# Counting edges on one NeuronCore: a block's digit sum in three pieces between places, its bytes parted one place sooner, GpSimd's staged edges in a ring of eight

## What is computed

```python
deg = jnp.maximum(segment_sum(ones, dst, num_segments=3125), 1.0)
deg_isqrt = deg ** (-0.5)
h = jnp.maximum(_layernorm(x), 0.0)
for i in range(10):
    agg = segment_sum(feat[src] * (d[dst] * d[src])[:, None], dst)
    feat_p = agg * 0.9 + 0.1 * h
    feat = feat_p * layer_reg[i] + (1.0 - layer_reg[i]) * feat
x = x + feat
h = jnp.maximum(_layernorm(x), 0.0)
for _ in range(4):
    m = (h @ W_msg.T + b_msg).reshape(n, 4, 128)
    r = segment_sum(m[src, edge_type], dst)
    h = gru_cell(r, h, w_ih, w_hh, b_ih, b_hh)
x = x + h
```

## Time and profile before

| | us |
|---|---|
| median of 3 runs | 2418.93 |
| lowest and highest of the 3 | 2417.05, 2979.36 |
| the profiled execution, its time | 2416.61 |
| its span in the profile | 2415.0 |
| one-hot places, first to last (in the span) | 39.35 to 423.54 |
| last digit sum ends | 439.87 |

### The profile page before, as it was taken

How to read it: one execution, slowest core, us unless ns; L and a number is a source line. 1 busy time by engine, 2 the same in 40 slices (tenths; PEclk the granted TensorE clock), 3 DMA queues, 4 the chain that set the end, 5 groups by cost and what they waited for, 6 DMA issues and landing times.

```text
span 2415.0 us, 40583 instructions
## 1 busy us (share of the span) xinstructions
PE 2159.3 (89%) x14377; PEld 1405.2 (58%) x14888; DVE 1384.7 (57%) x2714; ACT 505.5 (21%) x1122; POOL 235.7 (10%) x517
## 2 busy tenths in 40 slices
PE   4545555699999999999999999999999999999998
PEld 3223223599998989889544565444654446544465
DVE  8878778787777767787822347223463224542243
ACT  4877778400000000000300103000031000210010
POOL 4645555000000000000000000000000000000000
PEclk9565655699999999999999999999999999999999
DMA  2000000100000000005100000000000000010000
GB/s 77 22 33 22 22 33 22 50 2 1 2 2 2 2 2 1 2 1 151 47 1 1 1 1 1 1 1 1 1 1 1 1 1 1 1 27 1 1 1 28
DMA packets 23056, 34.26 MB, mean 14 GB/s; under 512 B 2573, under 2 KB 18939, under 8 KB 22466
## 3 DMA queue, kind: packets, MB, share of 16 engines
q1 hardware_dynamic: 19897, 30.56, 3.8%
q10 hardware_dynamic: 2944, 0.93, 0.2%
HBM read 18.04 MB, written 13.45 MB: 13 GB/s over the span
## 4 chain that ended last, share of the span: by engine, by line
PE 77%; DVE 9%; ACT 7%; issue 4%; ACTq 1%; DVEq 1%; POOL 0%; POOLq 0%; DMA 0%
PE ps L819 43%; PE ps L898 26%; PE ps L802 4%; ACT weighed L538 3%; PE ps L786 2%; ACT packed L531 2%; ACT words L520 1%; ACTq L511 1%; DVE marks L1093 1%; DVE dig L1121 1%; DVE big L1123 1%; PE ps L748 1%; DVEq L1080 1%; PE ps L883 1%; PE ps L704 1%
## 5 line engine op out<-in xcount | busy, mean ns | idle before, releaser
L819 PE MATMUL ps<-slots,m_parts 125*128 125x500 fp8e4 (+1 forms) x5600 | 1083.3, 353 | 1.5 <-DVE slots L1398 1.0
L819 PEld LDWEIGHTS ps<-slots,m_parts 125*128 125x128 f16 x5600 | 546.4, 98 | 487.5
L898 PE MATMUL ps<-parts,big 125*128 125x256 f16 x6125 | 669.5, 273 | 6.2 <-DVEq L1469 6.2
L898 PEld LDWEIGHTS ps<-parts,big 125*128 125x128 fp8e4 x6125 | 591.3, 98 | 63.5
L1398 DVE TENSOR_SCALAR slots<-big 128x3200 int32<-128x3200 int32 (+1 forms) x112 | 244.2, 2183 | 281.7 <-PE ps L819 281.6
L704 PE MATMUL ps<-hot_pair,weighed 125*128 125x228 f16 x1000 | 210.4, 359 | 180.8 <-ACT weighed L538 96.5
L704 PEld LDWEIGHTS ps<-hot_pair,weighed 125*128 125x128 f16 x1000 | 113.3, 120 | 277.9 <-ACT weighed L538 240.1
L538 ACT ACTIVATE weighed<-marks,win_w 125x128 f16<-125x128 f16 x625 | 195.6, 389 | 90.0 <-DVE marks L1093 89.0
L1526 DVE SCALAR_TENSOR_TENSOR r_parts<-ps,over,r_parts 128x500 f16<-128x500 f32 (+1 forms) x28 | 19.1, 684 | 229.7 <-ACT r_parts L615 229.7
L1533 DVE SCALAR_TENSOR_TENSOR gate_r<-ps,over,gate_r 128x500 f32<-128x500 f32 (+1 forms) x28 | 19.1, 681 | 226.6 <-PE ps L802 226.6
L477 ACT ACTIVATE rs<-rs 125x25 f32<-125x25 f32 (+3 forms) x5 | 1.1, 216 | 703.0 <-DVE rs L971 703.0
(11 more groups left out here) (204 smaller groups left out, 1328.8 us busy)
## 6 DMA issues: line engine op xcount, KB each, us to landing
packed_counts<-packed SPq DMA_DIRECT2D x16, 625.0 KB, 2.9
big<-packed_counts SPq DMA_DIRECT2D x4, 1600.0 KB, 7.6
big<-packed_counts SPq DMA_DIRECT2D x3, 1200.0 KB, 6.4
hd<-in_x SPq DMA_DIRECT2D x1, 1562.5 KB
x_again<-in_x SPq DMA_DIRECT2D x1, 1562.5 KB
big<-x_after_hops SPq DMA_DIRECT2D x1, 1400.0 KB
x_after_hops<-x SPq DMA_DIRECT2D x4, 224.0 KB
out<-big SPq DMA_DIRECT2D x4, 224.0 KB
```

The lines of the kernel that those rows point to most:

```text
L819: last = pe.matmul(ps[:, k % 2, 0:SIZES[k] * Q], m_parts[0:Q, a, h, t * F:(t + 1) * F], slots_f8[0:Q, t % 2, 0:SIZES[k], a, 0:Q], start=a ...
L898: last = pe.matmul(ps[:, n % RING, 0:2 * F], tot_f8[0:Q, c, a, :], both((parts0, parts1)[par], a), start=a == 0, stop=a == TILES - 1)
```

## The change

Three things are changed.

1. `sum_digits` is cut into three pieces, `part` (the wait for the lanes and two instructions), `add` (one instruction) and `place` (two). Within a block they are issued behind the places j = 5, 6 and 7, where all five instructions stood behind place 6. The last two blocks, summed behind all places, keep them in a row.
2. ACT parts the three lanes behind the places 2, 3 and 4, not 3, 4 and 5. In the last block the third lane moves into the block accordingly.
3. POOL's four tiles get eight buffers (`WINDOWS`). The first eight places are staged without a wait; from then on place q waits for PE to be done with place q - 8. POOL's loop has eight places in a pass, and the wait stands ahead of the register load. The one-hots keep their four buffers, which is why `onehots` and `weigh` now take two indices, b for these and v for the staged tiles.

```diff
--- before.py
+++ after.py
@@ -63,6 +63,7 @@
 TWOS, NIBBLES = 0x33333333, 0x0f0f0f0f
 BANKS = 8
 DEPTH = 4
+WINDOWS = 8
 ROUND = 4
 WA = 5
 WD = W - WA
@@ -169,10 +170,10 @@
-            win_key = sb("win_key", [128, DEPTH, W, 2], F16, b)
-            win_place = sb("win_place", [128, DEPTH, W, 2], F16, b)
-            win_f = sb("win_f", [128, DEPTH, W, 2], F16, b)
-            win_w = sb("win_w", [128, DEPTH, W], F32, b)
+            win_key = sb("win_key", [128, WINDOWS, W, 2], F16, b)
+            win_place = sb("win_place", [128, WINDOWS, W, 2], F16, b)
+            win_f = sb("win_f", [128, WINDOWS, W, 2], F16, b)
+            win_w = sb("win_w", [128, WINDOWS, W], F32, b)
             win_p = sb("win_p", [128, 2, W], F16, b)
             win_x = sb("win_x", [128, 3], F32, b)
             hot_pair_x = sb("hot_pair_x", [128, KP], F16, b)
@@ -395,7 +396,6 @@
 
             def stage_window(q, b):
                 lo = pool.value_load(windows[0:1, ds(q, 1)], min_val=0, max_val=NCH)
-                pool.wait_ge(s_hot_used, q + 1)
 
                 def twice(m):
                     return m.rearrange("p (w o) -> p w o", o=1).broadcast_to([CH, W, 2])
@@ -407,11 +407,15 @@
                                    q_off[0:CH, ds(q, 1)].rearrange("p (w o) -> p w o", o=1).broadcast_to([CH, W, 2]),
                                    ALU.subtract).then_inc(s_wst, 1)
 
-            with pool.Fori(0, Q // DEPTH) as i:
-                for j in range(DEPTH):
-                    stage_window(DEPTH * i + j, j)
-            for q in range(Q // DEPTH * DEPTH, Q):
-                stage_window(q, q % DEPTH)
+            for q in range(WINDOWS):
+                stage_window(q, q)
+            with pool.Fori(1, Q // WINDOWS) as i:
+                for j in range(WINDOWS):
+                    pool.wait_ge(s_hot_used, WINDOWS * (i - 1) + j + 1 + DEPTH)
+                    stage_window(WINDOWS * i + j, j)
+            for q in range(Q // WINDOWS * WINDOWS, Q):
+                pool.wait_ge(s_hot_used, q - WINDOWS + 1 + DEPTH)
+                stage_window(q, q % WINDOWS)
 
             pool.wait_ge(s_bnd, 1)
             pool.partition_all_reduce(mbound[:, 6:7], mbound[:, 5:6], 128, bass.bass_isa.ReduceOp.max).then_inc(s_bndr, 1)
@@ -532,22 +536,22 @@
                 if l == LANES - 1:
                     ins.then_inc(s_bytes, 1)
 
-            def weigh(q, b):
+            def weigh(q, b, v):
                 act.wait_ge(s_marks, q + 1)
                 for w in range(WA):
                     act.activation(weighed[0:CH, b, w, :], marks[0:CH, b, w, :], ACT.Copy,
-                                   scale=win_w[0:CH, b, w:w + 1]).then_inc(s_weighed, 1)
+                                   scale=win_w[0:CH, v, w:w + 1]).then_inc(s_weighed, 1)
 
             def block_of(turn, b, n, turn_before):
                 blk = 2 * turn + b
                 for j in range(n):
-                    weigh(BQ * blk + j, j % DEPTH)
+                    weigh(BQ * blk + j, j % DEPTH, j % WINDOWS)
                     if j >= 2:
                         evacuate(blk, b, j - 2)
                     elif turn_before is not None:
                         evacuate(2 * turn_before + 1 - b, 1 - b, BQ - 2 + j)
-                    if 3 <= j < 3 + LANES and turn_before is not None:
-                        part_lane(turn_before, 1 - b, j - 3, 16 * turn_before + BQ * (1 - b) + BQ - 1)
+                    if 2 <= j < 2 + LANES and turn_before is not None:
+                        part_lane(turn_before, 1 - b, j - 2, 16 * turn_before + BQ * (1 - b) + BQ - 1)
 
             block_of(0, 0, BQ, None)
             with act.Fori(0, (NB - 2) // ROUND) as i:
@@ -560,7 +564,6 @@
                 block_of(turn + 1, 0, BQ, turn)
             block_of(NB // 2 - 1, 1, Q - (NB - 1) * BQ, NB // 2 - 1)
             evacuate(NB - 1, 1, 3)
-            part_lane(NB // 2 - 1, 0, 2, BQ * (NB - 1) - 1)
             evacuate(NB - 1, 1, 4)
             for l in range(LANES):
                 part_lane(NB // 2 - 1, 1, l, Q - 1)
@@ -1075,7 +1078,7 @@
             dve.sem_inc(s_mp, 1)
             dve.sem_inc(s_ct, 1)
 
-            def onehots(q, b):
+            def onehots(q, b, v):
 
                 many = dve.value_load(windows[0:1, ds(q + MANY, 1)], min_val=0, max_val=NCH)
                 dve.wait_ge(s_wst, q + 1)
@@ -1091,12 +1094,12 @@
                     return m.rearrange("p w (o two) -> p w o two", o=1).broadcast_to([CH, count, n // 2, 2])
 
                 TT(by_two(marks[0:CH, b, :, :], 128), row(iota_row[0:CH, :], W, 128),
-                   each(win_place[0:CH, b, :, :], W, 128), ALU.is_equal).then_inc(s_marks, 1)
+                   each(win_place[0:CH, v, :, :], W, 128), ALU.is_equal).then_inc(s_marks, 1)
                 TT(by_two(hot_pair[0:CH, b, :, :], KP), row(iota_pair[0:CH, :], W, KP),
-                   each(win_key[0:CH, b, :, :], W, KP), ALU.is_equal).then_inc(s_pairs, 1)
+                   each(win_key[0:CH, v, :, :], W, KP), ALU.is_equal).then_inc(s_pairs, 1)
                 dve.wait_ge(s_marks, q + 1)
                 TT(by_two(weighed[0:CH, b, WA:W, :], 128), by_two(marks[0:CH, b, WA:W, :], 128),
-                   each(win_f[0:CH, b, WA:W, :], WD, 128), ALU.mult).then_inc(s_weighed_d, 1)
+                   each(win_f[0:CH, v, WA:W, :], WD, 128), ALU.mult).then_inc(s_weighed_d, 1)
                 with dve.If(many > 0):
                     lo = dve.value_load(windows[0:1, ds(q, 1)], min_val=0, max_val=NCH - 1)
                     with dve.Fori(0, many) as j:
@@ -1111,18 +1114,30 @@
                         TS(hot_pair_x[0:CH, :], iota_pair[0:CH, :], win_x[0:CH, 0:1], win_x[0:CH, 2:3],
                            ALU.is_equal, ALU.mult).then_inc(s_more, 1)
 
-            def sum_digits(blk, b):
-
-                dve.wait_ge(s_bytes, blk + 3)
+            def digit_pieces(blk, b):
+
                 x, low, high = packed[:, b, :].bitcast(I32), dig[:, 0, :], dig[:, 1, :]
                 low16, high16 = low.bitcast(DT.uint16), high.bitcast(DT.uint16)
-                TS(low, x, TWOS, None, ALU.bitwise_and)
-                step(TS(high, x, 2, TWOS, ALU.logical_shift_right, ALU.bitwise_and))
-                step(TT(low16, low16, high16, ALU.add))
-                step(TS(high16, low16, 1.0 + 1.0 / 16, None, ALU.mult))
-                step(TS(big1[:, :].bitcast(I32).rearrange("p (n q) -> p n q", q=32)[:, :, ds(2 * blk, 2)],
-                        high.rearrange("p (n q) -> p n q", q=2), NIBBLES, None, ALU.bitwise_and))
-                dve.sem_inc(s_digits, 1)
+
+                def part():
+                    dve.wait_ge(s_bytes, blk + 3)
+                    TS(low, x, TWOS, None, ALU.bitwise_and)
+                    step(TS(high, x, 2, TWOS, ALU.logical_shift_right, ALU.bitwise_and))
+
+                def add():
+                    step(TT(low16, low16, high16, ALU.add))
+
+                def place():
+                    step(TS(high16, low16, 1.0 + 1.0 / 16, None, ALU.mult))
+                    step(TS(big1[:, :].bitcast(I32).rearrange("p (n q) -> p n q", q=32)[:, :, ds(2 * blk, 2)],
+                            high.rearrange("p (n q) -> p n q", q=2), NIBBLES, None, ALU.bitwise_and))
+                    dve.sem_inc(s_digits, 1)
+
+                return part, add, place
+
+            def sum_digits(blk, b):
+                for piece in digit_pieces(blk, b):
+                    piece()
 
             def onehots_general(n, q, b, m):
 
@@ -1155,13 +1170,14 @@
                            ALU.is_equal, ALU.mult).then_inc(s_more_g, 1)
 
             for j in range(BQ):
-                onehots(j, j % DEPTH)
+                onehots(j, j % DEPTH, j % WINDOWS)
             def block_of(blk, b):
 
+                pieces = digit_pieces(blk, b)
                 for j in range(BQ):
-                    onehots(BQ * (blk + 1) + j, j % DEPTH)
-                    if j == BQ - 2:
-                        sum_digits(blk, b)
+                    onehots(BQ * (blk + 1) + j, j % DEPTH, j % WINDOWS)
+                    if j >= BQ - len(pieces):
+                        pieces[j - BQ + len(pieces)]()
 
             with dve.Fori(0, (NB - 2) // ROUND) as i:
                 steps.loop(i, 4 * ROUND)
@@ -1171,7 +1187,7 @@
             for blk in range((NB - 2) // ROUND * ROUND, NB - 2):
                 block_of(blk, blk % 2)
             for q in range(BQ * (NB - 1), Q):
-                onehots(q, q % DEPTH)
+                onehots(q, q % DEPTH, q % WINDOWS)
             sum_digits(NB - 2, 0)
             sum_digits(NB - 1, 1)
             dve.wait_ge(s_wout, 1)
```

## The result

The changed kernel takes 2444.64 us in the median of 4 runs (2441.45 to 2447.19), the kernel before 2419.47. The ratio is 1.0107, 95% interval 1.0087 to 1.0127: slower by 26 us or 1.1%, clear of noise and within 2%. (One of the four executions of the kernel before took 2979.36 us; it is a slow one, and the ratio leaves it out.) The profiled execution took 2441.45 us, its span is 2439.9. The forecast was 2442.

What follows compares the result with a forecast made beforehand. The counting's block period, a chain running to and fro between DVE and ACT, was taken to bound what the change touches. Period +27.6, straight-code pauses -0.7, ring -1.5, end -0.2 gave +25.2 us: 2442 us, range 2416 to 2452.

Steps and rivals of the forecast that it cites:

- The end of the counting decides: Counting ahead of PE's later stages: nothing overlaps it, so a microsecond there is a microsecond of the kernel.
- The lanes a place sooner trade places one for one: Each block: two ACT places ahead of DVE's wait become two DVE places behind it; 3.8 us leave and come back.
- The stretch: ACT's work before DVE may go on, from place 0's marks: 14.80 us, the old 18.58 less two places.
- Two pauses of 1.01 us: DVE, behind `part` and `add` in each block: the wait with the next place's register load behind it adds 1.01 us each.
- The row behind L1123: Kernel before: DVE's pause between a digit step and the next place, 1.01 us, taken as each new pause's size.
- The period: One block of the counting: 27.07 us instead of 25.10, 1.97 us more, 27.6 us over fourteen blocks.
- The ring: POOL's eight buffers: POOL never late in the counting, -1.5 us; the first block and the loop's edges unchanged.
- Edge and pause add up: DVE's two loop edges in the counting: pause and edge kept as a sum; overlapping would save 2 x 1.01 us.
- Hidden pauses: Rival: `part` and `add` cost only a step's 0.15 us; period 25.35, sum +1.1, 2418 us; 13 in 100.
- Lanes in time: Rival: third lane there by 11.4 us, DVE never waits; period 23.6, 22.7 us off, 2394 us; 5 in 100.
- A pause as long as an edge: Rival: each of 28 pauses lasts 2.95 us like DVE's loop edge; +54 us, 2496 us; 5 in 100.
- The sum: Whole kernel: 27.6 - 0.7 - 1.5 - 0.2 = +25.2 us on the profiled 2416.6 us.

Runs made afterwards that it cites:

- one-piece run: Changed kernel with all five digit instructions in a row behind place 5, earlier lanes and ring of eight kept: 2417.5 us, ratio 0.9987 against the kernel before.
- the ring's run: Kernel before with only POOL's eight buffers added, pieces and lanes as before: 2417.5 us, ratio 0.9988.
- the old lanes: Changed kernel with the three lanes behind places 3, 4 and 5 as before, pieces behind 5, 6 and 7: 2471.8 us, ratio 1.0216 against the kernel before.
- the load first: Changed kernel with the next place's register load issued ahead of the wait ending the first and second piece: 2419.9 us, ratio 0.9995 against the kernel before.
- the wait later: Changed kernel with the wait at a piece's end moved to the next piece's start: 2412.0 us, ratio 0.9970 against the kernel before.
- the run without pauses: As "the wait later", and the last digit instruction signals for itself, without DVE waiting for its end: 2396.6 us, ratio 0.9902 against the kernel before.
- later pieces: As "the run without pauses", with `part` behind place 7, `add` and `place` behind the next block's places 0 and 1: 2361.1 us, ratio 0.9753.

## Why the prediction was right

*The end of the counting decides.* Right: 24.2 of 24.9 us.

*The lanes a place sooner trade places one for one.* Shown by the one-piece run, which is the ring's run over again, and from the other side by the old lanes, +27 us for one place. The stretch was forecast at 14.80 us and is 14.55 in the block shown, since the blocks of before that it was worked out from have a slow second place (2.13 us for 1.89). The wait was forecast at 3.4 us and is 2.9 to 3.1: besides the shorter stretch, DVE takes 11.71 us for its six places (220.68 to 232.39), not 11.4. The prediction also says that ACT had eight places and three lanes in the old stretch. They were seven (place 7 and places 0 to 5); eight are DVE's. Its sum goes by the measured 18.58 us, so nothing rests on the count.

*Two pauses of 1.01 us.* They are 1.18 and 0.90 in the block shown, together 2.08 for 2.02, and 29.8 us in all where 27.6 were forecast. The row behind L1123 was the right one to go by: same instructions, same order. The cause was argued in the prediction and is shown now by "the load first" and "the wait later".

*The period.* Forecast 27.07, measured 26.89 and 27.09; between the starts of the first and the fourteenth `part` (69.72 and 426.91 us) lie 357.2 us, where it was 333.7.

*The ring.* Forecast -1.5 us. Alone, it measured -3 in the medians with an interval of -0.5 to -5, and -2.6 at the end of the counting. That it changes nothing in the first block was wrong, by 0.6 us. That the edge is no wait for POOL was right.

*Edge and pause add up* rather than overlap: 4.19 us, my sum was 3.96.

*The rivals.* Hidden pauses would have given 2418. They were in the open, 1.06 us in the mean. With the load ahead, 0.19 us are left. The Trainium skill (VectorE: DVE Perf Modes, The DRAIN you can't avoid) has a semaphore behind each VectorE instruction cost nothing extra. That nearly holds here for a wait by itself, 0.19 us; a wait with a register load behind it is a case that the section does not treat. Lanes in time would have given 2394: they were not. But that rival's price was right in kind: once the pieces start where the lanes are in time and the pauses are out, the period is DVE's work. A pause as long as an edge did not come about.

*The sum.* It was +25.2 us and the profiled executions differ by 24.8. That it is this close is partly luck: against the forecast, the gaps cost 2.2 us more and the edges 0.3 more, while the ring took 1.1 us more off (in its run alone) and the shorter stretch about 2.5 us, 0.25 us in some ten of the fourteen blocks (an estimate from the periods).

## What to carry to other kernels

Cutting a step into pieces between other work won little here while the waiting piece stayed where it was. With a wait at each cut it cost 27 us against one piece, and with the waits moved to where the result is next read it won 5.5 us (2412.0 for 2417.5). Each cut gave the engine one more wait for its own end, and what its sequencer had to do behind that wait, a register load here, came into the open. So put the wait where the result is next read and let the last instruction signal for itself. The larger gain, 35.5 us beyond the run without pauses, came when the waiting piece started later, where its input was finished anyway: ACT needed 14.55 us for its five places and three lanes, and DVE's eight places take 15.2.

When the profile names an engine as the one waited for, look at whether it had been idle for long: here it named PE for 28 waits and POOL for the loop's edges. The waits named PE went when DVE's own wait was moved, and the edge stayed when POOL had twice the buffers.

## What the runs showed of the hardware

- A register load behind a wait for the engine's own instruction left DVE idle for 0.73 to 1.31 us until the next instruction started (28 times in the changed kernel, 29.8 us). With the load ahead of the wait 0.19 us were left, and with the wait moved behind the next instructions nothing. The load itself took 0.30 us in some of these gaps and 0.58 in others, which I cannot explain.
- The edge of DVE's loop of four blocks took 2.95 and 2.84 us behind a one-hot in the kernel before, 4.19 and 4.06 behind a pause in the changed one, 2.73 and 2.53 behind `place` without a pause ("no pause"), and 5.71 and 6.25 behind `part` ("later pieces"), where I had expected one price. In the last, the chain has 2.58 and 3.11 us ahead of the jump's instructions, and another 2.15 and 2.19 us between them and the register load, where the others have 0.03. Why it grew stays open.
- POOL's small copies were stretched while DVE's one-hots ran. A copy of 125x16 that took 0.19 us while DVE waited (at 232.70 in the changed kernel) took 5.13 us from 225.15 to 230.28, and DVE's three instructions of a place kept their lengths beside it (0.68, 1.10 and 0.35 us). Why is not shown.
